# Stacked attention operands laid out dimension by dimension: three loads of 3, 2 and 1 rows each in place of six

## The reference

```python
q = (w @ Wq.T) ...; k = (w @ Wk.T) ...; v = (w @ Wv.T) ...   # (B, H, L, 16)
rp = (r @ Wr.T).reshape(2 * L - 1, H, 16)                    # r: table of sines and cosines
AC = einsum('bhid,bhjd->bhij', q + u_bias, k)
BD = rel_shift(einsum('bhid,hjd->bhij', q + v_bias, rp))     # row i moved left by L - 1 - i
attn = softmax((AC + BD) / sqrt(16))
out = einsum('bhij,bhjd->bhid', attn, v)
x = x + out
```

## Time and profile before

| what | us |
|---|---|
| median of 3 runs | 3201.2 (3196.62 to 3203.26) |
| the profiled execution, whole | 3208.71 |
| its span, first to last instruction | 3206.9 |
| PE busy in the span | 2906.8 |
| DVE busy | 2634.9 |
| ACT busy | 2496.0 |
| POOL busy (with its DMA issues) | 2310.1 |

### The profile page before, as it was taken

How to read it: one execution, slowest core, us unless ns; L and a number is a source line. 1 busy time by engine, 2 the same in 40 slices (tenths; PEclk the granted TensorE clock), 3 DMA queues, 4 the chain that set the end, 5 groups by cost and what they waited for, 6 DMA issues and landing times. The chain is left out here.

```text
span 3206.9 us, 110520 instructions
## 1 busy us (share of the span) xinstructions
PE 2906.8 (91%) x40768; PEld 2051.1 (64%) x40768; DVE 2634.9 (82%) x5042; ACT 2496.0 (78%) x3850; POOL 2310.1 (72%) x4135
## 2 busy tenths in 40 slices
PE   4655479999999999998999999999999999999955
PEld 1444237777777676776777776777767777777645
DVE  2555149899999899997999998999989999999976
ACT  2333368898888898987888898988888889889732
POOL 3333388888888878887878888888878888888800
PEclk8777679999999999999999999999999999999977
DMA  6233678888888878887888888888888888888831
GB/s 201 86 111 111 137 204 224 224 229 229 227 231 222 231 214 228 222 230 194 227 220 227 227 227 220 228 226 224 225 222 223 227 227 226 228 225 222 214 123 53
DMA packets 290222, 657.31 MB, mean 205 GB/s; under 512 B 189473, under 2 KB 256929, under 8 KB 272289
## 3 DMA queue, kind: packets, MB, share of 16 engines
q0 software_dynamic: 190960, 526.89, 62.1%
q1 hardware_dynamic: 98736, 123.38, 13.2%
HBM read 77.19 MB, written 46.14 MB: 38 GB/s over the span
## 5 line engine op out<-in xcount | busy, mean ns | idle before, releaser
L663 POOL DMA_DIRECT2D score<-score x3999 | 2178.4, 548 | 512.4 <-ACT score L902 442.3
L900 ACT COPY score<-pos_bank 128x512 f32<-128x512 f32 x2048 | 1104.2, 597 | 305.1 <-PE pos_bank L776 303.1
L910 ACT ACTIVATE score<-score,low 128x1024 f32<-128x1024 f32 x1024 | 1197.0, 1170 | 36.3 <-DVE low L963 30.2
L972 DVE COPY prob_t<-pt_bank 128x512 f32<-128x512 f32 x1792 | 1162.2, 684 | 7.9 <-PE pt_bank L842 4.0
L842 PE MATMUL pt_bank<-ident_sb,score 128*128 128x128 f32 x8192 | 1085.4, 275 | 10.8 <-issue 6.5
L842 PEld LDWEIGHTS pt_bank<-ident_sb,score 128*128 128x128 f32 x8192 | 953.5, 142 | 218.2 <-DVE prob_t L972 47.2
L963 DVE CUSTOM_DVE_ANT_0 score<-ac_bank,score 128x1024 f32<-128x1024 f32 x512 | 627.1, 1225 | 245.4 <-PE ac_bank L828 126.7
L776 PE MATMUL pos_bank<-pos,qv 96*32 96x512 bf16 (+15 forms) x12160 | 661.2, 317 | 49.9 <-DMA qv<-qv_parts 42.8
L963 DVE CUSTOM_DVE_ANT_0 score<-ac_bank,score,low 128x1024 f32<-128x1024 f32 x512 | 657.2, 1284 | 56.4 <-PE ac_bank L828 47.6
L856 PE MATMUL acc_bank<-prob_t,vs 128*32 128x128 f32 x16384 | 663.5, 279 | 3.5 <-issue 3.4
L828 PE MATMUL ac_bank<-ks,qu 96*128 96x512 bf16 x2048 | 623.9, 386 | 24.7 <-DVE low L963 24.4
(11 more groups left out here) (95 smaller groups left out, 995.6 us busy)
## 6 DMA issues: line engine op xcount, KB each, us to landing
score<-score POOLq DMA_DIRECT2D x3937, 129.5 KB, 5.1
pos<-pos_parts SPq DMA_DIRECT2D x96, 128.0 KB, 8.5
qv<-qv_parts SPq DMA_DIRECT2D x192, 64.0 KB, 7.2
ks<-k_parts SPq DMA_DIRECT2D x192, 64.0 KB, 7.3
qu<-qu_parts SPq DMA_DIRECT2D x192, 64.0 KB, 7.1
v_heads<-v_sb SPq DMA_DIRECT2D x8, 1024.0 KB, 7.3
vs<-v_heads SPq DMA_DIRECT2D x32, 256.0 KB, 8.0
pos_parts<-part SPq DMA_DIRECT2D x16, 384.0 KB, 3.0
```

The costliest lines, as they stand in the source:

```text
L663: pool.dma_start(shifted(odd, s, groups, 0), shifted(odd, s, groups, QUAD - 1 - s))\
L900: act.copy(score[:, at + f, c * BANK:(c + 1) * BANK], ring(m)[:, :]).then_inc(pos_out, 1)
L910: act.activation(cols, cols, ACT.Exp, bias=low[:, slot(k), NH - 1:NH], scale=-1.0)\
L972: dve.tensor_copy(prob_t[:, c, :], PT[c % 2][:, :]).then_inc(copied, 1)
```

## The change

The stack's rows change places. Run 0 holds the first three blocks, run 1 the next two, run 2 the last: `RUNS = ((0, 3), (3, 2), (5, 1))`, as first block and number. Within a run the rows go dimension by dimension: row 3d + s of run 0 holds dimension d of copy s. Both sides of a matmul are laid out alike, so the sum over the 96 rows has the same products. One transfer fetches a run: for keys and positions its source is read as (16 dimensions, parts, columns), for queries one part is read with a step of zero as often as the run has rows. So an operand is three transfers of 48, 32 and 16 rows (192, 128 and 64 KB; `pos` 384, 256 and 128 KB) where it was six, and carries the same bytes. The outermost dimension of each source has sixteen entries. `NLOAD` becomes 48.

The places in SP's order move too: `ks` to tiles 13, 15 and 17 of a head, `qu` to 19, 21 and 23, `qv` to 8, 10 and 12 (with its wait one tile earlier than before), `vs` from tile 12 to 14 with its wait, `pos` to 0, 4 and 14 tiles after its wait.

```diff
             block = c2.enter_context(nc.Block())
-            NLOAD = 16 * len(Q_PARTS)
+            RUNS = ((0, 3), (3, 2), (5, 1))
+            NLOAD = 16 * len(RUNS)
...
-                def load_head(dst, src, order, step, h, loaded, blocks):
+                def rows_of_run(i):
+
+                    return slice(RUNS[i][0] * DH, (RUNS[i][0] + RUNS[i][1]) * DH)
+
+                def load_queries(dst, src, step, h, loaded, blocks):
                     for i in blocks:
-                        sp.dma_start(dst[h % 2][i * DH:(i + 1) * DH, 0:L],
-                                     src[order[i], bass.ds(head(step, h) * DH, DH), :]).then_inc(loaded[h % 2], 16)
+                        part = src[i, bass.ds(head(step, h) * DH, DH), :].rearrange("d (o n) -> d o n", o=1)
+                        sp.dma_start(dst[h % 2][rows_of_run(i), 0:L], part.to_broadcast([DH, RUNS[i][1], L]))\
+                            .then_inc(loaded[h % 2], 16)
...
                 def load_ks(step, h, blocks):
-                    load_head(ks, k_parts, K_PARTS, step, h, ks_loaded, blocks)
+                    for i in blocks:
+                        sp.dma_start(ks[h % 2][rows_of_run(i), :],
+                                     k_parts[0:RUNS[i][1], bass.ds(head(step, h) * DH, DH), :]
+                                     .rearrange("s d n -> d s n"))\
+                            .then_inc(ks_loaded[h % 2], 16)
 
                 def load_pos(step, pair, blocks):
                     for i in blocks:
-                        sp.dma_start(pos[pair % 2][i * DH:(i + 1) * DH, :],
-                                     pos_parts[K_PARTS[i], bass.ds((step * (NT // PAIR) + pair) * DH, DH), :])\
+                        sp.dma_start(pos[pair % 2][rows_of_run(i), :],
+                                     pos_parts[0:RUNS[i][1], bass.ds((step * (NT // PAIR) + pair) * DH, DH), :]
+                                     .rearrange("s d n -> d s n"))\
                             .then_inc(pos_loaded[pair % 2], 16)
...
-                POS_FIRST, POS_BLOCK_AT = PAIR // 2 + 2, (0, 5, 10, 15, 20, 25)
-                KS_FIRST, KS_BLOCK_AT, QU_BLOCK_AT = 13, (0, 1, 2, 3, 4, 5), (6, 7, 8, 9, 10, 11)
-                QV_BLOCK_AT, VS_AT = (9, 10, 11, 12, 13, 14), 12
+                POS_FIRST, POS_BLOCK_AT = PAIR // 2 + 2, (0, 4, 14)
+                KS_FIRST, KS_BLOCK_AT, QU_BLOCK_AT = 13, (0, 2, 4), (6, 8, 10)
+                QV_BLOCK_AT, VS_AT = (8, 10, 12), 14
...
-                every = range(len(Q_PARTS))
+                every = range(len(RUNS))
```

4 lines of the change are left out of this document (2 added, 2 removed).

## The result

| | before | after |
|---|---|---|
| median, us | 3202.23 (3196.62 to 3213.71, 4 runs) | 3333.36 (3323.6 to 3343.38, 4 runs) |
| ratio | | 1.0404, 95% interval 1.0381 to 1.0426 |
| span of the profiled execution | 3206.9 | 3341.6 |
| PE busy in it | 2906.8 | 2950.7 |

The change costs 131 us. The forecast was +16, and the upper end of its range +41. The direction was right, the size was not.

What follows compares the result with a forecast made beforehand. PE's own work was taken to set the pace, with late shifts costing 1.04 us a head. Two heads +1.5 us, 14 pairs +21, start -3, rounded down to +16: 3217 us; own range 3208 to 3232, 8 in 10 3183 to 3242.

Steps and rivals of the forecast that it cites:

- (a): SP's stack loads: 336 transfers instead of 672, same bytes, taken as no gain or loss.
- (b): vs two tiles later, qv one earlier: lateness before heads' first tiles goes, -1.2 us for two heads.
- (d): Start of an even head: its train sees 960 KB instead of 640, lands at 7.8 us; +0.8 us for two heads.
- (c): Positions' wait, start of an odd head: burst makes the shift train land at 10.0 us; +1.9 us for two heads.
- (e): The first loads before PE begins: faster transfer over 48 partitions, -3 us once.
- R3: Rival: upper bounds of (c) and (d) hold, no gain at the start; 3240 us, chance 0.09.
- R1: Rival: loads get cheaper or drain in time, so the kernel is faster; 3184 us, chance 0.19.
- R4: Rival: vs comes too late and PE pays in 31 heads; 3248 us at 1 us each, chance 0.03.

Runs made afterwards that it cites:

- runs_old_places: The change's three transfers an operand and row order, but with the waits of the kernel before and transfers spread about as before: 3313.9 us, ratio 1.0329.
- strided_old_places: The kernel before with only the row order changed, each 16-row transfer going to every third (second) row of its run: 3204.0 us, ratio 0.9992.
- pieces_new_places: The change with its 48-row transfers cut by columns into three and its 32-row ones into two, at the change's places: 3244.2 us, ratio 1.0123.
- vs_later: The kernel before with only vs moved from tile 12 to 14 and qv one tile earlier: 3226.08 us, ratio 1.0068.
- no_positions: The change without the loads of pos after the first two pairs of heads: 3199.25 us, ratio 0.9971 to the kernel before.
- pos_two_later: The change with the positions' wait and first two pos transfers two tiles later: 3275.5 us.
- places_only: The kernel before's six 16-row transfers and block row order, issued at the change's places: 3295.7 us, ratio 1.0257.
- strided_six: The change's places and row order, but six 16-row transfers an operand: 3264.4 us, ratio 1.0181.
- the quarters: The kernel before with vs as four 32-row transfers at tiles 12 to 15: 3264.3 us; with column pieces too: 3321.6 us.
- pieces_old_places: The kernel before with the change's rows, 48-row transfers cut by columns into three and 32-row ones into two, at the old places: 3197.1 us, ratio 0.9968.

## Why the prediction was too small

**(a) Half as many transfers, taken as nothing: this step failed.** I priced a transfer by its bytes and looked only at whether SP had time to spare. It does. But in a burst each issue holds SP for 1.2 to 2.2 us at 64 or 128 KB, and in the change for 0.5 to 2.3 us at 64 to 384 KB, with no growth by size. With 64 KB an issue that is a throttle. The runs take it away: 110 us at about the old places, where nothing else moves much (runs_old_places against strided_old_places), and 89 at the new ones (the change against pieces_new_places). The rule on coalescing that was weighed there (the Trainium skill, DMA: Bandwidth & Descriptors, Rules for kernel authors) pointed to a gain; here fewer and larger transfers lost. No run here has a chain that waits for the small transfers themselves, so nothing is shown of that case.

**(b) `vs` later, -1.2 us for two heads: half right, and wrong in sum.** The trains in front of first tiles became punctual, and the distances there fell by 0.9 and 0.5 us, 1.4 together. I had put `vs` into the sum of (d) by its bytes, and they cost much more than a byte's price there: vs_later alone, +2.7 us in front of even heads' second group and 19 us in all.

**(c) The positions' burst, +1.9 us: right place, mis-sized.** The distances of an odd head's first three groups grew by 0.4, 6.2 and 0.8 us, 7.4 for two heads. The train landed 14.8 us after its last issue, in the close-up and on average over fourteen heads (15.7 at most), where 10.0 was forecast. The price of 0.44 us per 100 KB came from trains with 448 KB or less and was carried on to 1088 KB in a straight line. It does not go straight: 4.8 us more than the line gave. On top came what the term did not have at all, PE's pauses without a releaser and the lower clock behind them. That the burst is the cause is shown by no_positions and, at this place, by pos_two_later (27.2 to 20.2 us). There was a sign of the size in the earlier trace rows: the prediction read the 1.5 us between the two kinds of heads as the price of all stack loads, but the first of the two faster heads (2832.30 to 2913.96, 81.66 us) still loaded everything except `pos`.

**(d) The start of an even head, +0.8 us: right place, mis-sized.** +3.8 us. Its train landed 10.4 us after its last issue on average, where I took 7.8. places_only and strided_six show the same 24.0 and 24.6 us without the new shape, so here it is the meeting of `vs`, `ks` and `pos`, not the size of the issues. vs_later alone makes 2.7 of the 3.8 us.

**(e) The start, -3 us once:** about -2, by the first issue and the first matmul. Right in sign, and small.

**The sum.** -1.4 + 7.4 + 3.8 us are 9.8 for two heads, where I had 1.5. Fourteen pairs give 137, less 2 at the start: 135 of span, and 134.7 were measured.

**The rivals.** R3 was the nearest (upper bounds of (c) and (d), 3240), and decides "from where the positions' train lands more than 10.6 us after its last issue"; it landed at 14.8. Its bounds came from the same straight line. R1's own condition, cheaper transfers, did not hold (4.1 us per MB, 3.5 before). It had the right observation, "late in a burst SP is held about 2 us per transfer, so something does throttle it", and drew the wrong conclusion: I read the throttle as help for the change, though the change is what weakens it. R4 did not happen in the change, but did in the quarters.

**What stays open.** No run parts the share of the late shifts from that of PE's pauses and the low clock: the places are the same, and the pauses vary from burst to burst. That PE's pauses end with a packet of the instruction queue holds in all 273 cases; that a burst delays the packet was not tested apart. And why 192 KB in one issue hurts more than three issues of 64 KB at the same place has two readings that no run parts. One is SP's pace, shown above: the same bytes leave SP over 20 us in the pieces, over 8 in the runs. The other is what an engine serves in one go. In the packet lists 37% of the stack and `vs` rows of runs_old_places start within the 4 ns behind the end of another row of SP's queue, against 16% in strided_old_places. The lists do not name the engine, so it is a likely reading and not shown that the rows of one issue follow each other on an engine with no shift row between them. In pieces_old_places it is 37% as well, but with a third of the bytes in each row. The Trainium skill, DMA: Bandwidth & Descriptors, Queues, rings and completion order, says that an engine goes round its queues by packets of several descriptors, which agrees with this. If three rows of 8 KB go in one such packet, a shift row or an instruction packet has to wait for all three; no run measures it.

## What to carry to other kernels

Where small background loads share DMA engines with a stream that is waited for, the time that each issue holds the loading engine can be a throttle that the kernel leans on: before coalescing, count the KB that are issued in the few microseconds ahead of the waited landing, not the transfers. A price per byte holds only as far as the bytes of the rows it was read from. Moving a load out of one train puts it into another, so cost both places, and check what stood behind the wait that moved.

## What the hardware showed that I had not expected

- Matmuls stop in a DMA burst with no releaser in the profile: 29 pauses, 53 us between 700 and 2800, against 8 and 12.5 before. Each ends 2.2 to 3.6 us after a 16 KB packet of the instruction queue has started. Behind the pause in the close-up the granted clock is 0.55 in a window of 7 us with PE busy in it.
- Cutting a transfer of 48 rows by columns into three cost nothing and gave a little time against the kernel before: rows of 1.3 to 2 KB (`pos` 2.7 to 4 KB) and issues of about 64 KB (`pos` 128 KB) ran at 0.9968 of it (0.9952 to 0.9985).
- With transfers bunched, sixteen rows in adjacent partitions did worse than sixteen spread over 48: places_only 3295.7 us, strided_six 3264.4. With transfers apart there was no difference (0.9992). The Trainium skill, SBUF — State Buffer, Door 1: The DMA port swizzle, says that sixteen adjacent partitions reach fewer ports; the two bunched runs agree in direction, and no run here measures a port.
